# Decoder layer on one core: the last pair's projection between its value products, batched one-hots in the routing, bank sums ahead of the token list, first row turnings among the shared products

## The chip, the cores and the metric

One core of a Trainium2 chip runs the whole layer as one program. The metric is device microseconds from start to end of an execution. The core has five engines, each with its own instruction queue that runs in order: TensorE (PE), VectorE (DVE), ScalarE (ACT), GpSimd (POOL) and SyncE (SP, which here only starts DMAs). They meet at semaphores alone.

## The reference

1,024 tokens (4 batches of 256) of width 256 pass three parts; each adds to the stream x.

```
x = x + attn1(layernorm(x))                      # 16 heads of 16, causal
x = x + experts_by_token_id(layernorm(x))        # 4 experts, chosen by the token's id
h = layernorm(x)
a = rmsnorm(h, ln1_w)                            # part 3
q, k, v = a @ q_w.T, a @ k_w.T, a @ v_w.T        # 16 heads of 128, causal, scale 192**-0.5
hid = h + attention(q, k, v) @ o_w.T
x2 = rmsnorm(hid, ln2_w)
p = softmax(x2 @ gate_w.T)                       # 16 experts
w, i = top_k(p, 4);  w = w / sum(w)
routed = sum over k of w[k] * (silu(x2 @ g[i_k].T) * (x2 @ u[i_k].T)) @ w2[i_k].T    # inner 176
shared = (silu(x2 @ sg.T) * (x2 @ su.T)) @ sd.T  # inner 352
x = x + hid + routed + shared
```

## The kernel before

**Third attention.** The 16 heads go in 8 pairs. A pair `p` has 8 slots `u = 4a + b` (head `a` of the pair, batch `b`); `n = 8p + u` counts them. In slot `u`, TensorE's queue holds the scores of unit n+1, fills (the next head's q, k, v products), the value product of unit n-1 (`pe_pv3`, it needs the turned probabilities copied by ScalarE and VectorE, `act_pt3`, `dve_pt3`) and the turning of unit n. Most large products are done as three matmuls of split operands (high and low parts, `matmul3`, L226), so each operand has a "high" cast on ScalarE and a "low" subtraction on VectorE or GpSimd. The outputs of a head are copied out in two halves (`act_o3`, `dve_o3`; half 0 holds batches 0 and 1). `outputs3` says in which slot. The output projection of a pair (`pe_wo3`) has four groups of 12 matmuls, one for each 256 tokens, in banks `F_PS`, which VectorE adds to `acc` (`dve_wo3`). For all pairs but the last it is run in the next pair's slots; for the last pair it stands behind everything:

```
            pe_pv3(pe, 4 * H3 - 1, PAIRS - 1, 1, 3, H3 - 1, False)
            pe_wo3(pe, PAIRS - 1, BEFORE + PER_PAIR * (PAIRS - 1) + 4)
            pe_moe(pe)
```

In the last pair's slots, ScalarE and GpSimd also cast the first routed experts' weights (slots 1 to 3) and the shared expert's (slots 4 to 6).

**Norm and logits.** ScalarE squares `acc` by tiles, GpSimd makes the reciprocal root (`rms_gpsimd`), VectorE makes `h` (`dve_apply4`), SyncE stores h to DRAM as `x2d`, TensorE turns it (`transposes`, L197), ScalarE copies it twice (`act_hT4`, `hT_scalar`), and TensorE makes the logits (`pe_logits`, L1598).

**Shared expert and routing.** The shared expert has 6 steps `v` (two halves of the tokens by three chunks): `pe_gate_up` (12 matmuls of 512 columns), `act_silu`, `dve_shared`, `pe_down` (8 matmuls, L1588). The routing stands between them on VectorE: probabilities, the four largest, a prefix count on TensorE (`pe_prefix`), the place of each token in the list of its expert (`dve_places`), and for each of the four choices `k` two one-hot tensors (`dve_rows`): `Vk` (128 x 8 x 47, slot of the token, times a value) and `Rk` (128 x 8 x 128, row in the slot). `pe_list` multiplies them (8 products of 47 columns, L1620); their sum is the list of tokens, which `dve_tokens` turns into `tok` and `dst`. `Vk` lies in `acc`'s space and `Rk` in that of hT and h, so a step may start only when `acc` (by `dve_residual`) or h (stored) is done with. Order is written out by hand in `pe_moe`, `dve_moe` and `act_moe`.

**Routed slots.** 47 slots of 128 rows. GpSimd gathers the rows of slot s from `x2d` (L1468, ring of 8), TensorE turns them (`pe_turn`, L1631), ScalarE and VectorE copy them, then gate-up with the slot's expert (`G`, high and low), silu and product, turning, down product (L1661), ScalarE's copy into a ring of 4 (L1528), and GpSimd scatters the rows to `yb` (L1473). GpSimd's queue is ten gathers, then in turn gather s+10 and scatter s-3. Gather s waits for the turning of slot s-8. The 16 experts' low parts (`expert_low`, L1462, 128 x 704) are 5 on GpSimd ahead of the slots, 2 on VectorE ahead of them and 9 on VectorE in the slots. After the last scatter, `yb` is read back and summed with the weights.

SyncE's queue: experts 0 to 2, then 3 to 6 after the last pair's fills, the down weights `wd` (2.8 MB) after the last value product, the two stores of `x2d`, experts 7 to 10 after the last projection, experts 11 to 15 after the sixth shared down product.

Of the kernel before, what the change touches and what calls it, by code (L numbers as in the profile page):

```python
# [51 lines left out]
POOL_E = 5  # L52
RING = 8
TAIL_WARM = 36
MASKED = -1.0e30
# [4 lines left out]
RT_TOK = RT_POS + 2 * TOPK + 3  # L60
RT_ESL = RT_TOK + 4


def decoder_kernel(nc, x_in, tok_in, ctxT_in, wqT_in, wkT_in, wvT_in, woT_in, vec_in, bo_in, ffn_qk_in, ffn_v_in, ffn_o_in,
                   gate_in, sh_in, gu_in, wd_in, ln2_in, cst_in, ident_in, tri_in, out):
    with ExitStack() as ctx:
# [1091 lines left out]
        def pe_wo3(pe, p, fe_before, banks=range(4)):  # L1158

            pe.wait_ge(s_wol, p + 1)  # L1160
            pe.wait_ge(s_ol3, 4 * (p + 1))
            for g in banks:
                if g < 2:
                    pe.wait_ge(s_fe3, 2 * (fe_before - 1 + g))
                else:
                    pe.wait_ge(s_acc, 4 * p + g - 1)
# [19 lines left out]
        def pe_slot3(pe):  # L1186
            def slot(p, a, b, u, first, last, end):
# [19 lines left out]
                pe_transpose3(pe, n, u % 2, first and u < 2)  # L1207
            return slot
# [23 lines left out]
        def outputs3(p, a, b, first, last):  # L1232
# [3 lines left out]
            if last:  # L1236
                return {0: [(2 * p, 0, 0)], 2: [(2 * p, 0, 1), (2 * p + 1, 1, 0)]}.get(b, [])
# [12 lines left out]
        def act_slot3(act):  # L1250
            def slot(p, a, b, u, first, last, end):
# [7 lines left out]
                for head, a2, half in outputs3(p, a, b, first, last):  # L1259
                    if last and (a, b) == (1, 2):  # L1260
# [8 lines left out]
                if a == 1 and b == 2:  # L1269
                    act_wo3(act, p, first)  # L1270
                if last and 1 <= u < 4:
                    act_expert_high(act, u - 1)
                if last and 4 <= u < 4 + SC:
                    act_shared_high(act, u - 4)
            return slot

        def dve_slot3(dve):
            def slot(p, a, b, u, first, last, end):
# [12 lines left out]
                for head, a2, half in outputs3(p, a, b, first, last):  # L1291
                    dve_o3(dve, head, a2, half)
            return slot

        def pool_slot3(pool):
            def slot(p, a, b, u, first, last, end):
# [6 lines left out]
                if a == 1 and b == 2:  # L1303
                    pool_wo3(pool, p)
                if last and 1 <= u < 4:
                    expert_low(pool, u - 1, s_glp)
                if last and 4 <= u < 4 + SC:
                    pool_shared_low(pool, u - 4)
# [82 lines left out]
        s_glp = sem("s_glp")  # L1391
# [84 lines left out]
        def pool_moe(pool):  # L1476
            for e in range(3, POOL_E):
                expert_low(pool, e, s_glp)
# [51 lines left out]
        def act_diag(act, g, k):  # L1530

            act.wait_ge(s_rt, RT_ESL + 7)
            act.activation(diag[:, g, k, :], ident[:, :], ACT.Copy, scale=wkk[:, 2 * g + 1, k:k + 1]).then_inc(s_gh, 1)

        def act_moe(act):
# [6 lines left out]
            for v in range(2 * SC):  # L1542
                act_silu(act, v)
                if 1 <= v < 1 + len(GROUPS[2]):
                    act_expert_high(act, GROUPS[2][v - 1])
# [71 lines left out]
        def pe_list(pe, k):  # L1617
            pe.wait_ge(s_rt, RT_POS + 2 * k + 2)
# [5 lines left out]
        def pe_turn(pe, s):  # L1624
# [3 lines left out]
            else:  # L1628
                pe.wait_ge(s_am, 2 * SC - 1 + s)
# [34 lines left out]

# [550 lines left out]
```

## Time and profile before

| | |
|---|---|
| median of 3 runs (lowest, highest) | 673.27 us (669.9, 673.46) |
| profiled execution, span | 675.55 us, 673.7 us |
| busy: PE, DVE, ACT, POOL | 92%, 63%, 52%, 48% |
| mean granted clock of TensorE | 0.967 of 2.4 GHz |

Times in the rows count from the span's start, in us. A line number of a helper (L226, `matmul3`) stands for all its callers; the tiles' names tell them apart. The granted clock is a share of 2.4 GHz; 0.50 is 1.2 GHz, and a value between is a stretch that holds both. In the chain of waits, "issue" is time in which the engine waited for nothing that the profile shows. A number in brackets at the end of a timeline's row is idle time of the engine ahead of it, with what ended it.

### The profile page before, as it was taken

How to read it: one execution, taken by the hardware profiler on the slowest of the kernel's cores; microseconds unless marked ns; L12 is line 12 of the kernel's file. 1: busy time of each engine (PE TensorE's matmuls, PEld its weight loads, DVE VectorE, ACT ScalarE, POOL GpSimd, SP SyncE). 2: the span in 40 equal slices, each digit the busy share in tenths (PEclk: the TensorE clock that was granted, in tenths of full speed). 3: DMA queues.
4: the chain of work that ended last, by engine and by line, in shares of the span. 5: the costliest groups of instructions: out<-in, count | busy, mean ns of one | idle time of the engine just before them, and what ended most of it. 6: DMA issues, size and time to landing. Idle time of an engine off the chain costs nothing.

```text
span 673.7 us, 13478 instructions
## 1 busy us (share of the span) xinstructions
PE 620.3 (92%) x4132; PEld 541.5 (80%) x4132; DVE 424.4 (63%) x1134; ACT 350.5 (52%) x1120; POOL 324.0 (48%) x402
## 2 busy tenths in 40 slices
PE   8789888999889999999999999995879899999897
PEld 5567667888779999999999999995768799877775
DVE  4685887878556666666666666663694684444324
ACT  2567878443466656564756566665520165443330
POOL 7888887005433333333343433365102577777740
PEclk9899999999999999999999999996787999999899
DMA  5998930210000101020202020222820523333318
GB/s 172 219 135 209 157 36 1 83 65 2 1 0 3 62 1 62 0 62 0 62 0 62 0 62 0 79 90 49 189 84 21 158 93 101 104 102 103 102 65 310
DMA packets 27985, 52.36 MB, mean 78 GB/s; under 512 B 4235, under 2 KB 16011, under 8 KB 27851
## 3 DMA queue, kind: packets, MB, share of 16 engines
q1 hardware_dynamic: 22371, 38.79, 22.4%
q0 software_dynamic: 4512, 12.33, 5.7%
q10 hardware_dynamic: 1056, 0.66, 0.5%
q8 instruction: 25, 0.41, 0.3%
q14 instruction: 21, 0.17, 0.1%
HBM read 39.31 MB, written 12.45 MB: 77 GB/s over the span
## 4 chain that ended last, share of the span: by engine, by line
PE 63%; DVE 11%; POOL 8%; issue 6%; ACT 5%; DMA 5%; SPq 1%; ACTq 1%; DVEq 0%; POOLq 0%
PE bank L226 40%; PE bank L1661 4%; PE bank L1137 2%; DMA yb<-hx,dst 2%; POOL yb L1473 2%; PE bank L505 2%; DMA hx<-yb 2%; PE bank L1220 2%; POOL p L626 2%; PE bank L1588 2%; PE bank L1128 1%; POOL h L1468 1%; PE bank L488 1%; DMA x<-in 1%; PE bank L521 1%
## 5 line engine op out<-in xcount | busy, mean ns | idle before, releaser
L279 POOL TENSOR_TENSOR p_sb<-p_sb,prec 128x256 f32<-128x256 f32 (+1 forms) x128 | 62.3, 508 | 139.4 <-DVE prec L273 139.4
L266 ACT ACTIVATE p_sb<-bank,nmax 128x256 f32<-128x256 f32 x64 | 30.4, 475 | 89.3 <-DVE nmax L259 89.3
L616 ACT ACTIVATE p<-bank,nmax 128x256 f32<-128x256 f32 (+1 forms) x128 | 52.6, 426 | 20.8 <-DVE nmax L608 20.1
L626 POOL TENSOR_TENSOR p<-p,rec 128x512 f32<-128x512 f32 x48 | 50.2, 1055 | 17.2 <-DVE rec L621 16.9
L1473 POOL DMA_INDIRECT yb<-hx,dst x47 | 47.7, 1015 | 20.1 <-issue 11.6
L226 PE MATMUL bank<-hTh,w3h 128*128 128x512 f32 x128 | 53.0, 414 | 1.8 <-DVE hTl L220 1.8
L226 PE MATMUL bank<-G,xTh 128*128 x188 | 51.5, 357 | 0.0
L273 DVE RECIPROCAL prec<-psum_ 128x2 f32<-128x2 f32 x64 | 10.6, 166 | 63.3 <-ACT p_sb L268 63.3
L226 PE MATMUL bank<-hTh,w3l 128*128 128x512 f32 x128 | 50.4, 394 | 0.0
L226 PE MATMUL bank<-hTl,w3h 128*128 128x512 f32 x128 | 50.0, 391 | 0.0
L1661 PE MATMUL bank<-wd,hx 88*128 x188 | 49.2, 385 | 0.0
L1468 POOL DMA_INDIRECT xg<-x2d,tok x24 | 23.4, 975 | 50.5 <-DVE tok L1826 38.3
L1528 ACT ACTIVATE hx<-bank 128x256 f32<-128x256 f32 x47 | 18.1, 385 | 52.1 <-DMA yb<-hx,dst 38.8
L608 DVE TENSOR_REDUCE nmax<-bank 128x2 f32<-128x512 f32 (+1 forms) x48 | 32.7, 682 | 13.9 <-PE bank L491 13.8
L1873 DVE COPY hx<-bank 88x256 f32<-88x256 f32 x47 | 19.8, 421 | 34.0 <-PE bank L1653 33.0
L226 PE MATMUL bank<-wv3h,hTh 128*128 128x256 f32 x128 | 37.3, 292 | 2.8 <-DVE k3l L1107 2.8
L226 PE MATMUL bank<-wo3h,ctxTh 128*128 128x256 f32 x128 | 38.3, 299 | 1.5 <-issue 1.5
L226 PE MATMUL bank<-wo3l,ctxTh 128*128 128x256 f32 x128 | 36.8, 288 | 0.0
L226 PE MATMUL bank<-wo3h,ctxTl 128*128 128x256 f32 x128 | 36.8, 287 | 0.0
L505 PE MATMUL bank<-ident,p 128*128 128x128 f32 x192 | 30.5, 283 | 5.9 <-POOL p L626 5.6
L226 PE MATMUL bank<-wv3l,hTh 128*128 128x256 f32 x128 | 35.6, 278 | 0.0
L226 PE MATMUL bank<-wv3h,hTl 128*128 128x256 f32 x128 | 35.6, 278 | 0.0
(263 smaller groups left out, 2113.7 us busy)
## 6 DMA issues: line engine op xcount, KB each, us to landing
Gf<-in SPq DMA_DIRECT2D x16, 352.0 KB, 5.3
qk<-staged SPq DMA_DIRECT2D x36, 128.0 KB, 6.7
staged<-qk SPq DMA_DIRECT2D x8, 512.0 KB, 9.7
w<-in SPq DMA_DIRECT2D x16, 256.0 KB, 3.2
wd<-in SPq DMA_DIRECT2D x1, 2816.0 KB
wv<-in SPq DMA_DIRECT2D x9, 256.0 KB, 3.6
wo<-in SPq DMA_DIRECT2D x9, 256.0 KB, 2.6
hx<-yb SPq DMA_DIRECT2D x2, 1024.0 KB, 10.2
```

The costliest lines, as they stand in the source:

```text
L226: mm = pe.matmul(out, lhs[a], rhs[b], start=(start and i == 0), stop=(stop and i == 2), skip_group_check=check)
L266: act.activation(p_sb[:, k, 0:256], S_PS[k][:, 0:256], ACT.Exp, bias=nmax[:, k, 0:1], accum_out=sums[0]).then_inc(u.ex, 1)
L279: pool.tensor_tensor(p, p, r.to_broadcast(p.shape), ALU.mult).then_inc(u.pn, 1)
L505: mm = pe.transpose(ps[:, (k * job.keys // P + kb) * P:(k * job.keys // P + kb + 1) * P], job.probs(n % 2)[:, k, kb * P:(kb + 1) * P], ide ...
L608: dve.tensor_reduce(nmax1[:, n % 2, job.stats], job.scores(), AX.X, ALU.max, negate=True).then_inc(job.nm, 1)
L616: act.activation(job.probs(n % 2)[:, k, :], job.scores()[:, k, :], ACT.Exp, bias=nmax1[:, n % 2, i:i + 1], accum_out=sums1[:, n % 2, i:i + ...
L626: pool.tensor_tensor(p, p, rec1[:, n % 2, job.stats].unsqueeze(2).to_broadcast(p.shape), ALU.mult)\
L1468: pool.indirect_dma_start(RG[s % RING], None, x2d[:, :], bass.IndirectOffsetOnAxis(ap=tok[:, s:s + 1], axis=0))\
L1473: pool.indirect_dma_start(yb[:, :], bass.IndirectOffsetOnAxis(ap=dst[:, s:s + 1], axis=0), ysb[:, s % 4, :], None)\
L1528: act.activation(ysb[:, s % 4, :], YS_PS[s % 2][:, 0:D], ACT.Copy).then_inc(s_oe3, 1)
L1661: mm = pe.matmul(YS_PS[s % 2][:, 0:D], aT[:, s % 2, c, :], wd[:, bass.ds(e, 1), c, :].rearrange("p a n -> p (a n)"), start=(c == 0), stop= ...
L1873: dve.tensor_copy(aT[:, s % 2, :, :], AT_PS[s % 2][0:DC, 0:2 * P].rearrange("p (c k) -> p c k", c=2))\
```

## The change

- Last pair: `pe_wo3` group 0 stands between the turning of the last unit and its value product, group 1 behind that product, groups 2 and 3 after them. Groups 0 and 1 wait for three output halves and not for four.
- Last pair: the copy of head 15's half 0 moves from slot 6 to slot 7, the wo3 casts from slot 6 to slot 5, the shared casts from slots 4 to 6 to slots 1 to 3. The routed experts' high casts leave the slots: one behind the last output, the others behind the silus of the shared expert (`EARLY_HIGH`).
- All 16 low parts of the routed experts are on VectorE: three ahead of the slots, then one in each of slots 0 to 12.
- `dve_rows`: two batched comparisons and one batched product in place of 16 operations.
- `residual` 0 to 3 move: 0 and 1 behind `dve_apply4`, 2 and 3 among the one-hot steps. `hT_vector` of the second half stands ahead of the second logits. The first bank sums (`dve_shared_out`) and the slots' experts stand ahead of `dve_tokens`.
- `pe_turn` 0 and 1 stand among the last shared products and wait for silu 4 and 5; the wait for the last bank sums moves to the first slots' down products.
- 7 and 6 matmuls of zeros (bf16, 512 columns) stand ahead of the two turnings of h.
- The order of the down and list products changes: before gu0 gu1 prefix gu2 dn0 list0 list1 gu3 list2 list3 dn1 dn2 gu4 dn3 gu5 dn4 dn5 turn0 turn1; after gu0 gu1 prefix dn0 gu2 dn1 list0 gu3 list1 dn2 list2 list3 dn3 gu4 gu5 turn0 dn4 turn1 dn5.

The diff, cut to its core (the count bases of `s_rt` move with the third operation of each row step):

```diff
-POOL_E = 5
+EARLY_HIGH = {0: (1, 2), 1: (3, 4), 2: (5, 6), 3: (7, 8, 9, 10)}
+AHEAD = 3
...
+HEAD_WARM = (7, 6)
...
-RT_TOK = RT_POS + 2 * TOPK + 3
-RT_ESL = RT_TOK + 4
+RT_ESL = RT_POS + 3 * TOPK + 4
+RT_TOK = RT_ESL + 3
...
-        def pe_wo3(pe, p, fe_before, banks=range(4)):
+        def pe_wo3(pe, p, fe_before, banks=range(4), outputs=4):
...
-            pe.wait_ge(s_ol3, 4 * (p + 1))
+            pe.wait_ge(s_ol3, 4 * p + outputs)
...
-                if g < 2:
+                if g < 2 and fe_before is not None:
...
+                if end:
+                    pe_wo3(pe, p, None, range(0, 1), outputs=3)
...
         def pe_pv3(pe, n, p, a, b, head, nofree):
...
-                return {0: [(2 * p, 0, 0)], 2: [(2 * p, 0, 1), (2 * p + 1, 1, 0)]}.get(b, [])
+                return {0: [(2 * p, 0, 0)], 2: [(2 * p, 0, 1)], 3: [(2 * p + 1, 1, 0)]}.get(b, [])
...
         def act_o3(act, head, a, i):
...
-                    if last and (a, b) == (1, 2):
+                    if last and a == 1 and b >= 2:
...
-                if a == 1 and b == 2:
+                if a == 1 and b == (1 if last else 2):
...
-                if last and 1 <= u < 4:
-                    act_expert_high(act, u - 1)
-                if last and 4 <= u < 4 + SC:
-                    act_shared_high(act, u - 4)
+                if last and 1 <= u < 1 + SC:
+                    act_shared_high(act, u - 1)
...
         def dve_slot3(dve):
...
+                if last and u == 1:
+                    dve.wait_ge(s_lb, DONE + 32)
+                    dve.tensor_copy(lowb[:, :], cst[:, C_LOWB:C_LOWB + P]).then_inc(s_lb, 1)
+                    dve.memset(onesb[:, :], 1.0).then_inc(s_lb, 1)
...
         def pool_slot3(pool):
...
-                if a == 1 and b == 2:
+                if a == 1 and b == (1 if last else 2):
...
-                if last and 1 <= u < 4:
-                    expert_low(pool, u - 1, s_glp)
-                if last and 4 <= u < 4 + SC:
-                    pool_shared_low(pool, u - 4)
+                if last and 1 <= u < 1 + SC:
+                    pool_shared_low(pool, u - 1)
...
         def pool_moe(pool):
-            for e in range(3, POOL_E):
-                expert_low(pool, e, s_glp)
...
-                if 1 <= v < 1 + len(GROUPS[2]):
-                    act_expert_high(act, GROUPS[2][v - 1])
+                for e in EARLY_HIGH.get(v, ()):
+                    act_expert_high(act, e)
...
-                pe.wait_ge(s_am, 2 * SC - 1 + s)
+                pe.wait_ge(s_gs, 2 * SC - 1 + s)
...
         def pe_slot_gate_up(pe, s, e):
...
-            if s >= 2:
-                pe.wait_ge(s_am, SHARES + s - 1)
-            if s < POOL_E:
-                pe.wait_ge(s_glp, s + 1)
-            elif s < E3:
-                pe.wait_ge(s_gld, s - POOL_E + 1)
+            pe.wait_ge(s_am, SHARES + s - 1)
+            if s < E3:
+                pe.wait_ge(s_gld, s + 1)
...
+            else:
+                pe.wait_ge(s_yx, ADDED)
...
+        def pe_zeros(pe, times, ps):
+            for i in range(times):
+                pe.matmul(ps[:, :], zb[:, 0:P], zb[:, :], start=True, stop=True, skip_group_check=True)
         def pe_moe(pe):
...
+                pe_zeros(pe, HEAD_WARM[g], bank[0])
...
+            pe_down(pe, 0)
...
-            pe_down(pe, 0)
+            pe_down(pe, 1)
...
+            pe_gate_up(pe, 3)
...
-            pe_gate_up(pe, 3)
+            pe_down(pe, 2)
...
-            pe_down(pe, 1)
-            pe_down(pe, 2)
+            pe_down(pe, 3)
...
-            pe_down(pe, 3)
...
+            pe_turn(pe, 0)
...
+            pe_turn(pe, 1)
...
-            pe.wait_ge(s_yx, ADDED)
-            pe_turn(pe, 0)
-            pe_turn(pe, 1)
...
-            for i in range(TAIL_WARM):
-                pe.matmul(SUM_PS[1][:, :], zb[:, 0:P], zb[:, :], start=True, stop=True, skip_group_check=True)
+            pe_zeros(pe, TAIL_WARM, SUM_PS[1])
...
-            for t in range(NT):
-                one = dve.tensor_scalar(Vk[k][:, t, :], cst[:, C_SLOT:C_SLOT + SLOTS], pb[:, t, k:k + 1], val[:, t, k:k + 1],
-                                        ALU.is_equal, ALU.mult)
-            one.then_inc(s_rt, 1)
-            for t in range(NT):
-                one = dve.tensor_scalar(Rk[k][:, t, :], cst[:, C_ROW:C_ROW + P], rowf[:, t, k:k + 1], None, ALU.is_equal)
-            one.then_inc(s_rt, 1)
+                dve.wait_ge(s_yx, 3)
+            dve.tensor_tensor(Vk[k], cst[:, C_SLOT:C_SLOT + SLOTS].unsqueeze(1).to_broadcast([P, NT, SLOTS]),
+                              pb[:, :, k:k + 1].to_broadcast([P, NT, SLOTS]), ALU.is_equal).then_inc(s_rt, 1)
+            dve.tensor_tensor(Rk[k], cst[:, C_ROW:C_ROW + P].unsqueeze(1).to_broadcast([P, NT, P]),
+                              rowf[:, :, k:k + 1].to_broadcast([P, NT, P]), ALU.is_equal).then_inc(s_rt, 1)
+            dve.wait_ge(s_rt, RT_POS + 3 * k + 1)
+            dve.tensor_tensor(Vk[k], Vk[k], val[:, :, k:k + 1].to_broadcast([P, NT, SLOTS]), ALU.mult).then_inc(s_rt, 1)
...
         def dve_tokens(dve):
...
         def dve_moe(dve):
...
-            for g in range(2):
-                dve_logits(dve, g)
+            dve_logits(dve, 0)
+            hT_vector(dve, n4, 1)
+            dve_logits(dve, 1)
...
-            hT_vector(dve, n4, 1)
...
+            dve_shared(dve, 1)
...
+            dve_residual(dve, 2)
...
-            dve_shared(dve, 1)
...
+            dve_shared(dve, 2)
...
-            dve_shared(dve, 2)
-            dve_tokens(dve)
...
+            dve_residual(dve, 3)
...
+            dve_tokens(dve)
+            dve_weights(dve)
+            expert_low(dve, 0, s_gld)
...
-            dve_weights(dve)
+            expert_low(dve, 1, s_gld)
...
-            for e in range(POOL_E, 7):
-                expert_low(dve, e, s_gld)
+            dve_turned(dve, 0)
+            expert_low(dve, 2, s_gld)
+            dve_turned(dve, 1)
...
-            dve_turned(dve, 0)
-            dve_turned(dve, 1)
...
-                if 7 + s < E3:
-                    expert_low(dve, 7 + s, s_gld)
+                if AHEAD + s < E3:
+                    expert_low(dve, AHEAD + s, s_gld)
...
-            for e in GROUPS[1]:
-                act_expert_high(act, e)
+            act_expert_high(act, 0)
...
-            pe_wo3(pe, PAIRS - 1, BEFORE + PER_PAIR * (PAIRS - 1) + 4)
+            pe_wo3(pe, PAIRS - 1, None, range(1, 2), outputs=3)
+            pe_wo3(pe, PAIRS - 1, None, range(2, 4))
...
+            dve_wo3(dve, PAIRS - 1, range(0, 1))
...
-            dve.wait_ge(s_lb, DONE + 32)
-            dve.tensor_copy(lowb[:, :], cst[:, C_LOWB:C_LOWB + P]).then_inc(s_lb, 1)
-            dve.memset(onesb[:, :], 1.0).then_inc(s_lb, 1)
-            for g in range(4):
+            for g in range(1, 4):
...
-                if g < 2:
-                    dve_residual(dve, g)
...
-                if not g:
-                    dve_residual(dve, 2)
-            dve_residual(dve, 3)
+            for g in range(2):
+                dve_residual(dve, g)
```

## Rows read from the trace of the kernel before

**Rows 1.** The page's costliest groups: ... | busy us, mean ns | idle us, releaser.

```profile
L1528 ACT ACTIVATE hx<-bank 128x256 f32<-128x256 f32 x47 | 18.1, 385 | 52.1 <-DMA yb<-hx,dst 38.8
```

**Rows 2.** Stretches: us, busy time of the five engines, granted clock, DMA share, GB/s.

```profile
458.00:461.40 3.40, 0.09 (x1) 0.01 (x1) 2.08 (x5) 2.62 (x7) 2.47 (x4) 0.89 0.00 0
...
467.50:475.00 7.50, 7.47 (x48) 7.27 (x48) 3.61 (x7) 4.53 (x14) 4.13 (x4) 0.77 0.70 144
...
482.00:487.00 5.00, 5.00 (x35) 4.96 (x35) 1.78 (x5) 2.56 (x5) 0.00 (x0) 0.74 0.82 178
...
503.20:512.00 8.80, 8.79 (x30) 7.64 (x30) 7.70 (x34) 0.00 (x0) 0.00 (x0) 0.51 0.01 2
```

**Rows 3.** The chain of waits, last pair to last projection: start us, us, what.

```profile
458.33 0.97 ACT ctxTh L1242 x2
459.31 0.52 ACT wo3h L1072
459.83 0.52 ACT wsh L1493
...
466.03 1.46 issue
467.49 7.50 PE bank L226 x48
```

**Rows 4.** The same chain, norm, turning and logits.

```profile
479.06 0.49 DVE h L1720
479.60 2.52 PE bank L197 x8
482.12 4.81 PE bank L1598 x32
```

**Rows 5.** The same chain, products of the shared expert and lists.

```profile
512.06 3.64 PE bank L1620 x32
...
523.53 1.73 PE bank L1588 x8
525.26 2.76 PE bank L226 x12
```

**Rows 6.** Timeline of VectorE: start us, us, engine, line, operation, count, idle before.

```profile
496.52 1.80 DVE L1813 TENSOR_SCALAR acc<-cst,pb,val 128x47 f32<-128x47 f32 x8
498.24 1.65 DVE L1817 TENSOR_SCALAR hT<-cst,rowf 128x128 f32<-128x128 f32 x8
...
516.20 0.19 DVE L1826 TENSOR_SCALAR tok<-tok 128x47 int32<-128x47 int32 x1
...
525.98 0.68 DVE L1851 TENSOR_TENSOR prod<-key,srt 128x512 f32<-128x512 f32 x1
...
542.00 0.88 DVE L1462 TENSOR_TENSOR G<-Gf,G 128x704 fp32r<-128x704 f32 x1
```

**Rows 7.** Timeline of GpSimd, gathers and scatters.

```profile
517.28 1.22 POOL L1468 DMA_INDIRECT xg<-x2d,tok  x1 [38.25 <-DVE tok L1826]
...
533.76 0.94 POOL L1468 DMA_INDIRECT xg<-x2d,tok  x1 [5.56 <-PE bank L1631]
...
542.09 1.60 POOL L1468 DMA_INDIRECT h<-x2d,tok  x1 [1.33 <-PE bank L1631]
544.00 1.71 POOL L1473 DMA_INDIRECT yb<-hx,dst  x1 [0.30 <-issue]
...
630.90 0.99 POOL L1473 DMA_INDIRECT yb<-hx,dst  x1 [0.30 <-issue]
...
642.06 0.97 POOL L1473 DMA_INDIRECT yb<-hx,dst  x1 [1.31 <-ACT hx L1528]
644.33 0.97 POOL L1473 DMA_INDIRECT yb<-hx,dst  x1 [1.30 <-ACT hx L1528]
...
653.25 0.97 POOL L1473 DMA_INDIRECT yb<-hx,dst  x1 [0.31 <-issue]
```

**Rows 8.** Timeline of TensorE near the end.

```profile
651.93 7.93 PE L1707 MATMUL bank<-zb 128*128 128x512 bf16 x36
```

More of the change, by code:

```diff
@@ L1390, in decoder_kernel @@
         s_gh = sem("s_gh")
-        s_glp = sem("s_glp")
         s_gld = sem("s_gld")
@@ L1530, in act_diag @@
         def act_diag(act, g, k):
-            act.wait_ge(s_rt, RT_ESL + 7)
+            act.wait_ge(s_rt, RT_TOK + 7)
             act.activation(diag[:, g, k, :], ident[:, :], ACT.Copy, scale=wkk[:, 2 * g + 1, k:k + 1]).then_inc(s_gh, 1)
@@ L1617, in pe_list @@
         def pe_list(pe, k):
-            pe.wait_ge(s_rt, RT_POS + 2 * k + 2)
+            pe.wait_ge(s_rt, RT_POS + 3 * k + 3)
             for t in range(NT):
@@ L1830, in dve_slot_experts @@
             dve.tensor_tensor(ends[:, :], base[:, :], nslot[:, :], ALU.add).then_inc(s_rt, 1)
-            dve.wait_ge(s_rt, RT_TOK + 1)
+            dve.wait_ge(s_rt, RT_ESL - 3)
             dve.tensor_tensor(ecmp[:, :, :], ends[0:1, :].unsqueeze(1).to_broadcast([1, SLOTS, E3]),
@@ L1834, in dve_slot_experts @@
                .then_inc(s_rt, 1)
-            dve.wait_ge(s_rt, RT_TOK + 2)
+            dve.wait_ge(s_rt, RT_ESL - 2)
             dve.tensor_reduce(esum[:, :], ecmp[:, :, :], AX.X, ALU.add).then_inc(s_rt, 1)
-            dve.wait_ge(s_rt, RT_TOK + 3)
+            dve.wait_ge(s_rt, RT_ESL - 1)
             dve.tensor_scalar(esl[:, :], esum[:, :], float(E3 - 1), None, ALU.min).then_inc(s_rt, 1)
@@ L1842, in dve_weights @@
             dve.scalar_tensor_tensor(chosen[:, :, :], left[:, :, :], 0.0, pr[:, :, :], ALU.is_lt, ALU.mult).then_inc(s_rt, 1)
-            dve.wait_ge(s_rt, RT_ESL + 1)
+            dve.wait_ge(s_rt, RT_TOK + 1)
             dve.tensor_reduce(sums[:, :], chosen[:, :, :], AX.X, ALU.add).then_inc(s_rt, 1)
-            dve.wait_ge(s_rt, RT_ESL + 2)
+            dve.wait_ge(s_rt, RT_TOK + 2)
             dve.reciprocal(sums[:, :], sums[:, :]).then_inc(s_rt, 1)
-            dve.wait_ge(s_rt, RT_ESL + 3)
+            dve.wait_ge(s_rt, RT_TOK + 3)
             dve.tensor_tensor(chosen[:, :, :], chosen[:, :, :], wide(sums[:, :]), ALU.mult).then_inc(s_rt, 1)
@@ L1852, in dve_weights @@
                               ALU.is_equal).then_inc(s_rt, 1)
-            dve.wait_ge(s_rt, RT_ESL + 5)
+            dve.wait_ge(s_rt, RT_TOK + 5)
             dve.tensor_tensor(eq, eq, chosen[:, :, :].unsqueeze(2).to_broadcast(shape), ALU.mult).then_inc(s_rt, 1)
-            dve.wait_ge(s_rt, RT_ESL + 6)
+            dve.wait_ge(s_rt, RT_TOK + 6)
             dve.tensor_reduce(wkk[:, :, :], eq, AX.X, ALU.add).then_inc(s_rt, 1)
```

## The prediction, made before the changed kernel was run

> **What bounds the kernel now.** I read the page first. TensorE is the busiest engine of the span, so its work and its clock matter most, but late in the kernel another engine is the one that others wait for: ScalarE's copies of the routed results sat idle 52.1 us, 38.8 of them until a scatter had landed [rows 1]. Then I cut the part that the diff touches into stretches and read TensorE's busy time beside the granted clock [rows 2]. TensorE stands almost still from 458.0 to 461.4 us, and the clock then falls from 1.00 to 0.50 (2.4 to 1.2 GHz). It is at 0.77 over the projection, low again in the logits' stretch (0.74 over 482 to 487), and at half rate in the stretch with the list products (0.51), where TensorE was busy throughout. The chain of waits says what TensorE waited for, and the timelines of VectorE and GpSimd give durations and the order of their queues.
>
> The chain reads thus. The last pair's ScalarE queue holds two output copies, the wo3 cast and a wsh cast ahead of the copy of the next turned probabilities [rows 3]; TensorE waits for that copy. After the last value product it waits again, 1.46 us, for the last output's low part, and only then starts the 48 matmuls of the projection [rows 3]. Then come the norm, its turning and the logits [rows 4], the shared expert mixed with the routing [rows 5], the one-hots on VectorE [rows 6], and 94 gathers and scatters on GpSimd [rows 7]. From 544.00 to 630.90 GpSimd issues one scatter and one gather in turn, without a pause beyond its own issue time, 33 pairs in 86.9 us, 2.63 us each. That is the pace of the routed slots: TensorE, which does one in 2.27 us where it sets the pace (642.06 to 644.33), waits through ScalarE for the scatters [rows 1, 7]. The question is thus when GpSimd's first gather starts, how soon its queue runs without a pause, and what stretches it.
>
> **Part 1, end of the last pair.** Before, TensorE's idle time from 458.0 ends at 461.4 [rows 2]. The wo3 cast goes to slot 5, the wsh cast to slot 3, and one of the two output copies behind the turned copy: 1.6 us leave ScalarE's queue ahead of it [rows 3]. The first output's low part stays ahead of it on VectorE (0.69), so I take 1.1 us: the product starts at 460.3. In slot 5 the cast waits for the last group of the previous projection, which TensorE issues ahead of that slot's value product; the exponential ahead of the cast ends later, so I cost the move at nothing (1.4 us, one group, if that cover is gone). The 48 matmuls took 7.50 us at a mean clock of 0.77 [rows 2, 3], so a group of 12 is 1.44 us at full clock and 2.6 at half. Group 0 now fills the time in which TensorE waited for the last turned copy, group 1 the 1.46 us for the last output. The idle stretch shrinks only from 3.4 to 2.3 us, so I still expect one dip, ending sooner because TensorE is then busy without a gap. With one dip of about 3.4 us, at half rate, the order is: value product to 461.5, turning to 462.2, group 0 to 464.5, last product to 465.4, then three groups of 1.44: end at 469.7 instead of 475.0. Gain 5.3. Bounds: 6.5 with no dip, 1.0 with half clock throughout.
>
> **Part 2, norm to logits.** From the projection's end the second `h` tile group comes after 4.05 us in both kernels, through VectorE, ScalarE and GpSimd, and the turning ended 7.1 us after it, the logits 11.9 us after it [rows 4]. 13 matmuls of zeros (0.22 us each at full clock, 36 took 7.93 near the end [rows 8]) fill TensorE's pauses; they cost nothing while they end before `h` comes, at most 0.3 us in front of the first turning, which nobody waits for. If they hold the clock, turning ends with the last `h` at 6.2, and 32 logit matmuls take 4.81 x 0.74 = 3.6 us: 9.8 instead of 11.9. Gain 2.1; bound 0. The residual sums leave VectorE's queue ahead of `h`, which came out of its wait for rstd anyway.
>
> **Part 3, logits to token list.** Count from the logits' end, L (486.9 before). At full clock a gate-up product is 2.76 us, a down product 1.73, a list product 3.64 / 2 = 1.82 [rows 5]. Places ended at L+9.6 and start after the prefix behind two gate-ups, so this stays. One row step cost 1.72 + 1.64 = 3.36 us of VectorE (8 + 8 instructions) [rows 6]. A two-input operation of 512 columns took 0.68 us and of 704 columns 0.88, so 1.04 us for each 1,000 columns and 0.15 fixed [rows 6]. The batched step is 376 + 1,024 + 376 columns: 0.54 + 1.21 + 0.54 = 2.3 us. That is 1.07 less, four times 4.3. VectorE's new queue is: shared 0.65, rows 2.3, residual 0.7, rows 2.3, rows 2.3, shared 0.65, rows 2.3, shared 0.65, residual 0.7, two bank sums 1.3, slot experts 2.2, tokens 0.6. From L+9.8 that is L+26.5. TensorE's new order ends the last list at L+24.4 if the clock holds, so VectorE sets the tokens, and emptying the banks plus the slot experts ahead of them costs 1.4 us of it. Before it was 516.39, L+29.5 [rows 6]. Gain 3.0. Bounds: 4.4 if the tokens came straight behind the last list, and 0 if the clock dips twice (1.7 us each).
>
> **Part 4, tokens to first scatter.** Before: first gather 0.9 us behind the tokens, eight gathers, then 5.56 us of idle time until the first row turning, 1.35 and 1.33 us for the next ones, scatter 0 at 544.00, 27.6 us behind the tokens [rows 7]. After: turns 0 and 1 stand among the shared products, at about L+31.7 and L+33.6, before GpSimd needs them (it reaches gather 8 at L+38). So it runs 14 gathers at 1.27 us (0.97 and 0.30 of issue) [rows 7] without a pause: 0.9 + 17.8. TensorE's first slot starts at L+35.8, and slot output 0 is ready in time. To this come stretched issues: the issue of 542.09 took 1.60 us while VectorE's cast of 542.00 ran, against 0.97 [rows 6, 7]. All sixteen low parts are now on VectorE, three ahead of the slots and thirteen in them; before it had eleven, nine of them in the slots. In the trace four of the nine casts inside the slots met an issue so, 0.65 us each (the one at 544.00 is another): 0.29 us per cast. Up to scatter 0 that is ten casts' worth with the weights' operations, 3.2 us. Sum 21.9 instead of 27.6. Gain 5.7; bounds 8.9 (no stretch) and 2.3 (each meets one). GpSimd loses its five casts, which it did while it had nothing else to issue; TensorE waited for none of them: nothing. If that cover is gone the price is VectorE's 0.88 us for each, once ahead of the slots.
>
> The GPSIMD Engine Reference (section 8, Key points) of the Trainium skill says that GpSimd shares its SBUF interface with VectorE and contends with VectorE instructions that have two SBUF inputs; the cast is one, and the trace agrees in four of nine cases. Taken for every cast, that rule is rival (e).
>
> **Part 5, slots.** 33 pairs as before, with eight casts in place of six: 87.5 instead of 86.9, a loss of 0.6. From scatter 33 to the last took 22.35 us and the rest of the kernel 20.4 [rows 7]; both stay. SP's last expert loads wait for the same count of down products and come nearer to the first slots; what they delay on ScalarE is hidden behind GpSimd's pace.
>
> **Sum.** 5.3 + 2.1 + 3.0 + 5.7 - 0.6 = 15.5 us off a span of 673.7. One more dip in the list products at even odds takes 0.8. The profiled run took 675.55, the median is 673.27; 673.3 - 14.7 = **658.5**.
>
> **Rivals.** (a) The forecast, 0.52, 653 to 664. (b) TensorE's clock stays at half: the dip at 461 lasts through the projection (-4.3), the zeros do not hold it (-2.1), two more dips lie in the lists (-2.6 beyond the 0.8): 667.5. For it speaks that 467.5 to 475 and 503 to 512 are low in the trace although TensorE was busy [rows 2]; 0.14. (c) TensorE's shorter way is worth more than I count, the issues rarely meet a cast and no dip comes: 5.3 to 6.5 in part 1, 3 us in part 4, 0.8: 653; 0.15. (d) The batched one-hots are not shorter, because a broadcast operand slows them: 4.3 us later tokens, 662.8. Against it: the 0.68 us row has two broadcast operands [rows 6]; 0.06. (e) Each of 16 casts stretches an issue by 0.65: 10.4 instead of 4.6, 664.3; 0.08. (f) Slower: the small-column list products spread among the others keep the clock at 1.2 GHz through all shared products. 34 us of TensorE's work at full clock become 64, 29 us more; with the other gains kept, the kernel is slower by 14, 687. It turns at 15 us of added time, that is half clock over 30 of these us. Against it: the gate-up product of 525.26 ran at full clock, 12 matmuls in 2.76 us, close behind list and down products [rows 5]; 0.05.
>
> Chances: faster by over 0.5% (3.4 us, about what this measurement can tell from no change) 0.94, within 0.02, slower 0.04. The range takes (c) with 4 us below and (b) above: 649 to 668.
>
> **What would show it.** The projection's first 12 matmuls between the last turning and the last value product; its end near 470; the logits' end near 479.5; one-hot operations of 0.54 and 1.21 us; tokens at about 506; GpSimd without idle time from the first gather; scatter 0 near 528; scatter 33 near 615. Wrong would be: the first value product not before 461, a granted clock of 0.50 over most of the shared products, tokens behind the last down product, or slots paced by TensorE at 2.27 us.

## The result, and the profile after

| | before | after |
|---|---|---|
| median (lowest, highest), 4 runs each | 673.37 us (669.9, 674.96) | 652.66 us (651.88, 655.19) |
| ratio of the times, 95% interval | | 0.9716 (0.9687 to 0.9745) |
| profiled execution, span | 675.55, 673.7 us | 652.61, 650.7 us |
| mean granted clock | 0.967 | 0.991 |
| busy: PE, DVE, ACT, POOL | 92%, 63%, 52%, 48% | 94%, 65%, 54%, 48% |

The kernel is 20.7 us faster; 14.7 were forecast. In the ratios here and below, two runs at a lower clock than the rest (683.27 us of before, 704.92 us of turns_behind_2) are left out. The page's group that answers to [rows 1] is unchanged, so the routed slots run as they did, and the gain lies ahead of them and in the kernel's last part:

```profile
L1529 ACT ACTIVATE hx<-bank 128x256 f32<-128x256 f32 x47 | 18.1, 384 | 52.0 <-DMA yb<-hx,dst 39.2
```

The stretches after (us, busy time of PE, PEld, DVE, ACT, POOL, granted clock, DMA share, GB/s), beside [rows 2]:

```profile
458.00:459.00 1.00, 0.60 (x4) 0.63 (x5) 0.85 (x3) 0.00 (x0) 0.00 (x0) 0.80 0.00 0
459.00:460.00 1.00, 1.00 (x7) 1.00 (x6) 0.00 (x0) 0.00 (x0) 0.00 (x0) 0.50 0.00 0
...
462.00:463.00 1.00, 1.00 (x10) 1.00 (x10) 0.44 (x1) 0.00 (x0) 0.00 (x0) 0.99 0.00 0
...
463.00:475.00 12.00, 11.63 (x79) 8.90 (x80) 7.61 (x16) 8.08 (x24) 2.63 (x4) 1.00 0.76 176
475.00:480.00 5.00, 5.00 (x33) 4.50 (x33) 4.45 (x19) 2.88 (x5) 0.00 (x0) 1.00 0.83 177
495.00:504.00 9.00, 9.00 (x62) 8.37 (x62) 8.65 (x20) 2.51 (x4) 1.17 (x1) 1.00 0.00 1
609.00:630.90 21.90, 20.71 (x118) 17.04 (x118) 7.90 (x23) 8.20 (x25) 13.91 (x15) 1.00 0.24 88
```

One dip is left, the forecast one at 458 to 462. The projection's remainder, the logits and the list products, which [rows 2] show at 0.77, 0.74 and 0.51, run at 2.4 GHz. The chain of waits after, from the product of the last unit but one to the turnings of the rows, beside [rows 3, 4, 5]:

```profile
458.40 0.80 PE bank L228 x3
...
460.26 2.62 PE bank L228 x15
...
464.53 0.03 issue
464.56 3.12 PE bank L228 x24
...
469.63 0.41 POOL ve L185
...
471.15 1.69 DVE h L1723 x4
...
473.65 3.57 PE bank L1599 x32
...
497.67 3.50 PE bank L1621 x32
...
508.48 0.22 PE bank L1632 x2
508.70 1.73 PE bank L1589 x8
```

The 15 products of 460.26 are projection group 0 and the last value product; groups 2 and 3 (464.56) follow with 0.03 us of issue where before there were 1.46. TensorE's timeline has the idle time ahead of 458.40:

```profile
458.40 0.37 PE L228 MATMUL bank<-pt3h,v3h 128*128 128x256 f32 x1 [2.13 <-DVE pt3f L1152]
```

VectorE's timeline of one row step, and of the tokens, beside [rows 6]:

```profile
487.15 0.54 DVE L1816 TENSOR_TENSOR acc<-cst,pb 128x376 f32<-128x376 f32 x1
487.61 1.22 DVE L1818 TENSOR_TENSOR hT<-cst,rowf 128x1024 f32<-128x1024 f32 x1
488.75 0.54 DVE L1821 TENSOR_TENSOR acc<-acc,val 128x376 f32<-128x376 f32 x1
489.21 0.68 DVE L1735 TENSOR_TENSOR x<-x,acc 128x512 f32<-128x512 f32 x1
...
501.32 0.18 DVE L1825 TENSOR_TENSOR dst<-bank,cst 128x47 int32<-128x47 f32 x1
...
501.76 0.19 DVE L1829 TENSOR_SCALAR tok<-tok 128x47 int32<-128x47 int32 x1
```

GpSimd's timeline, first gather, the stretched gathers, first scatter, scatter 33 and the last one, beside [rows 7]:

```profile
502.83 1.28 POOL L1471 DMA_INDIRECT xg<-x2d,tok  x1 [31.72 <-DVE sums L1849]
504.42 0.95 POOL L1471 DMA_INDIRECT xg<-x2d,tok  x1 [0.30 <-issue]
...
518.35 1.41 POOL L1471 DMA_INDIRECT h<-x2d,tok  x1 [0.30 <-issue]
520.06 1.62 POOL L1471 DMA_INDIRECT h<-x2d,tok  x1 [0.31 <-issue]
521.99 1.00 POOL L1476 DMA_INDIRECT yb<-hx,dst  x1 [0.30 <-issue]
...
609.65 0.99 POOL L1476 DMA_INDIRECT yb<-hx,dst  x1 [0.30 <-issue]
...
630.00 0.97 POOL L1476 DMA_INDIRECT yb<-hx,dst  x1 [0.30 <-issue]
```

The pauses of 5.56 and 1.33 us ahead of the ninth and later gathers [rows 7] are gone.

Some more rows of before are needed for the comparison. TensorE's timeline shows how it came to the list stretch:

```profile
499.94 2.13 PE L1620 MATMUL bank<-acc,hT 128*128 128x47 f32 x16 [2.43 <-DVE hT L1817]
```

Behind that stretch, its last two lists (512.06 to 515.70 [rows 5]) and the down products after them ran without a gap, and the clock fell once more:

```profile
512.00:515.70 3.70, 3.70 (x34) 3.70 (x33) 0.00 (x0) 1.28 (x2) 0.00 (x0) 0.94 0.00 0
515.70:520.40 4.70, 4.70 (x17) 3.87 (x17) 1.27 (x4) 0.00 (x0) 2.51 (x3) 0.68 0.09 28
```

The chain of waits has GpSimd's first operation of the norm:

```profile
476.93 1.01 POOL ve L183
```

And one stretch shows the clock of before near the end:

```profile
634.00:640.00 6.00, 6.00 (x28) 5.30 (x29) 2.20 (x7) 2.16 (x7) 3.57 (x5) 0.72 0.23 91
```

### The profile page after: what moved, and what is told of

Read it like the earlier page. It is cut to its first block, busy times and chain, and to the rows that moved or that the text cites. A ratio compares the mean times of both kernels' runs of the same rounds, so it can differ in the third digit from the quotient of the medians.

```text
span 650.7 us, 13445 instructions
## 1 busy us (share of the span) xinstructions
PE 608.7 (94%) x4135; PEld 531.4 (82%) x4145; DVE 422.9 (65%) x1087; ACT 349.3 (54%) x1120; POOL 315.3 (48%) x397
## 4 chain that ended last, share of the span: by engine, by line
PE 61%; DVE 11%; POOL 10%; issue 6%; ACT 6%; DMA 5%; another core or an unknown queue 1%; SPq 1%; ACTq 1%; DVEq 0%; POOLq 0%
PE bank L228 40%; PE bank L1661 3%; POOL yb L1476 3%; PE bank L1139 2%; DMA hx<-yb 2%; PE bank L507 2%; POOL p L628 2%; PE bank L1589 2%; DMA yb<-hx,dst 2%; PE bank L1224 2%; POOL xg L1471 1%; PE bank L1130 1%; POOL h L1471 1%; DVE ctxTl L1251 1%; PE bank L523 1%
## 5 line engine op out<-in xcount | busy, mean ns | idle before, releaser
L618 ACT ACTIVATE p<-bank,nmax 128x256 f32<-128x256 f32 (+1 forms) x128 | 52.5, 424 | 20.1 <-DVE nmax L610 19.5
L228 PE MATMUL bank<-G,xTh 128*128 x188 | 50.0, 348 | 0.0
L1471 POOL DMA_INDIRECT xg<-x2d,tok x24 | 24.7, 1028 | 38.7 <-DVE sums L1849 31.7
L1870 DVE TENSOR_TENSOR hx<-hx,bank 128x176 f32<-128x176 f32 x47 | 15.6, 332 | 31.1 <-ACT hx L1523 30.9
```

The source lines that it names most:

```text
L228: mm = pe.matmul(out, lhs[a], rhs[b], start=(start and i == 0), stop=(stop and i == 2), skip_group_check=check)
L618: act.activation(job.probs(n % 2)[:, k, :], job.scores()[:, k, :], ACT.Exp, bias=nmax1[:, n % 2, i:i + 1], accum_out=sums1[:, n % 2, i:i + ...
L1471: pool.indirect_dma_start(RG[s % RING], None, x2d[:, :], bass.IndirectOffsetOnAxis(ap=tok[:, s:s + 1], axis=0))\
L1870: dve.tensor_tensor(amx[:, s % 2, :], sg[:, s % 2, :], GS_PS[s % 2][:, INNER:GW], ALU.mult).then_inc(s_am, 1)
```

## The experiments

Each kernel is the changed one with one edit (combo has two), timed beside the kernel before on the same chip. They ran in three sessions; lowest and highest are over all runs of a kernel.

| session | kernel | median us (lowest, highest) | ratio to before (95%) |
|---|---|---|---|
| 1 | before | 673.22 (670.05, 683.27) | |
| 1 | control | 653.4 (652.81, 654.45) | 0.9719 (0.9684, 0.9753) |
| 1 | old_slots | 653.49 (651.9, 653.71) | 0.9709 (0.9673, 0.9745) |
| 1 | no_zeros | 655.62 (654.05, 657.48) | 0.9739 (0.9704, 0.9774) |
| 1 | old_rows | 657.85 (657.59, 658.93) | 0.9783 (0.9748, 0.9817) |
| 2 | before | 690.97 (689.36, 696.0) | |
| 2 | proj_behind | 678.47 (677.24, 681.76) | 0.9831 (0.9791, 0.987) |
| 2 | turns_behind | 675.56 (673.46, 677.43) | 0.9768 (0.973, 0.9806) |
| 2 | no_slot_casts | 675.91 (673.94, 678.38) | 0.979 (0.975, 0.983) |
| 2 | ring8 | 674.47 (672.69, 677.28) | 0.9771 (0.9731, 0.9811) |
| 3 | before | 691.09 (688.0, 693.73) | |
| 3 | control_2 | 676.9 (674.91, 678.03) | 0.9793 (0.9766, 0.9819) |
| 3 | combo | 674.74 (673.32, 677.63) | 0.9772 (0.9742, 0.9803) |
| 3 | turns_behind_2 | 673.86 (672.14, 704.92) | 0.9754 (0.9725, 0.9783) |
| 3 | no_slot_casts_2 | 677.12 (675.43, 679.55) | 0.9813 (0.9786, 0.9841) |

In sessions 2 and 3 every kernel took longer, before by 17.8 us and the changed one by 23.5. The change was thus worth 20 us in session 1 and 14 in session 3. In the profiles the extra time lies in the routed slots: the first gather comes at 503.28 in control_2 (502.37 in control), the last scatter at 655.30 (629.39). The stages ahead of the slots can therefore be compared between sessions; the slots only within one. Session 2 had no control.

**control** is the changed kernel again, to see what repeats.

> The changed kernel once more, as the measure for the others of this call. Span 650 to 653.5 us, ratio to before 0.969 to 0.975; one clock dip of about 3.4 us near 459, none in the shared products, tokens near 502, scatter 0 near 522, scatter 33 near 609.7.

It repeats in time. But the turning of unit 62, the last but one of the last pair, comes at 455.43 in control, 455.78 in the first profile, 456.21 in control_2, 456.86 in proj_behind and 459.27 in no_zeros, though nothing ahead of it differs. So a stage's start moves by up to 3.8 us from profile to profile, and a difference of that size between the starts of a stage in two profiles is no effect. The length of one stretch repeats far better: from unit 0's turning in the last pair to unit 62's it is 20.02 us in control (435.41 to 455.43), 20.03 in the first profile and 20.04 in no_zeros.

**old_slots** puts the shared casts back into slots 4 to 6:

```diff
-                if last and 1 <= u < 1 + SC:
-                    act_shared_high(act, u - 1)
+                if last and 4 <= u < 4 + SC:
+                    act_shared_high(act, u - 4)
```

(the same for GpSimd's `pool_shared_low`).

> The changed kernel with the shared expert's casts back in slots 4 to 6 of the last pair. Theory: these casts stood in front of the turned copies there, so the last value products come 1.5 to 2.5 us later and so does everything behind them; the kernel is 2 us slower than the control. Rival: the 1.9 us by which slot 7 came earlier than I forecast is owed to the routed experts' casts leaving slots 1 to 3; then this costs under 0.5 us.

The median did not move, and my theory for the unforecast part of part 1's gain fell. In the trace the stretch from unit 0's turning to the projection's end is 0.5 us longer than in control (32.32 and 31.80 us). The rival named the routed experts' casts, which left slots 1 to 3. No run puts them back, but from unit 0's turning to unit 62's the changed kernel is only 0.5 us shorter than before (20.03 and 20.55), so both moves of casts together can't be worth more there.

**no_zeros** takes the 13 matmuls of zeros out.

```diff
-HEAD_WARM = (7, 6)
+HEAD_WARM = (0, 0)
```

> The changed kernel without the 13 matmuls of zeros. Theory: the zeros hold TensorE's clock; without them it falls to 0.50 over the second turning and most of the logits, which end 2 to 2.5 us later, and the kernel is 2 to 2.5 us slower than the control. Rival: h now comes soon enough and the clock stays; under 0.5 us.

Its chain and its stretches:

```profile
475.54 2.12 PE bank L199 x7
477.66 4.18 PE bank L1599 x32
```

```profile
475.00:477.00 2.00, 1.78 (x6) 1.17 (x7) 2.00 (x6) 0.15 (x1) 0.00 (x0) 0.60 0.70 165
477.00:479.50 2.50, 2.50 (x17) 2.50 (x16) 1.16 (x3) 2.25 (x5) 0.00 (x0) 0.64 1.03 250
```

The dip is back in the stage where [rows 2] have it, and the logits take 4.18 us and not 3.57. Of the twelve other profiles of the changed kernel and its variants, all with the zeros, none has a granted clock below 1.00 between 468 and 500 us. From the last 24 projection products to the logits' end it is 13.84 us (468.01 to 481.85), in control 12.66 (464.08 to 476.74): 1.2 us. The medians differ by 2.2, and the intervals of the two ratios overlap; the other 1.0 is not assigned.

**old_rows** goes back to 16 operations for each row step (the `dve.tensor_scalar` lines of the diff).

> The changed kernel with the one-hots made by 16 operations a step as before (the third signal of a step is given with the second). Theory: a step takes 3.36 us instead of 2.06, VectorE sets the tokens, which come 4.5 to 6 us later; the clock may dip in the lists for 1.7 more; the kernel is 5 to 7 us slower than the control. Rival: TensorE's list products set the tokens and hide VectorE's steps; then under 1.5 us.

A row step takes 3.27 us of VectorE (487.74 to 491.01) and not 2.06. Four of them make 4.8; the way from the logits' end to the first gather grew from 25.63 to 30.50 us, 4.9, and the medians by 4.45. In this kernel TensorE waits for VectorE once more, 0.39 us at 504.8, behind its last two lists, and its clock falls there:

```profile
504.00:508.50 4.50, 4.11 (x14) 3.32 (x14) 4.22 (x14) 0.00 (x0) 0.19 (x1) 0.62 0.00 0
```

**proj_behind** puts all four projection groups behind the last value product (VectorE's additions follow):

```diff
-                if end:
-                    pe_wo3(pe, p, None, range(0, 1), outputs=3)
...
-            pe_wo3(pe, PAIRS - 1, None, range(1, 2), outputs=3)
-            pe_wo3(pe, PAIRS - 1, None, range(2, 4))
+            pe_wo3(pe, PAIRS - 1, None, range(0, 4))
```

> The changed kernel with all four groups of the last projection behind the last value product, as before. Theory: TensorE waits again about 1.1 us for the last turned copy and 1.5 us for the last output, and the clock stays at 0.50 for one stretch more; from the turning of unit 62 to the projection's end it takes 2.6 to 4.5 us longer, and the kernel is as much slower than the control. Rival: the gain in this stretch came from the shorter queue of casts alone; then under 1 us.

Its chain has before's wait again, to the hundredth [rows 3]:

```profile
463.20 1.46 issue
464.66 7.33 PE bank L228 x48
```

From the turning (456.86) to the projection's end it is 15.1 us, in control 11.8 (455.43 to 467.20): 3.4 us, and the same 3.4 to the first gather (50.35 and 46.94). That includes the clock, which stays at 0.50 until 467 us and in control until 461. The median lies 2.6 to 4.0 us above those of the three other variants of its session.

Its profile shows something else that control's does not, a dip right behind the last two lists (502.04 to 505.54), with TensorE busy throughout:

```profile
502.00:505.00 3.00, 3.00 (x30) 3.00 (x29) 2.90 (x6) 0.00 (x0) 0.00 (x0) 1.00 0.01 3
505.00:509.00 4.00, 4.00 (x14) 3.34 (x14) 3.72 (x12) 0.00 (x0) 1.49 (x2) 0.57 0.00 0
```

**turns_behind**, and once more **turns_behind_2**, put the first two row turnings behind the shared products, where they wait for the last bank sums (VectorE's queue is reordered to match).

```diff
-            pe_turn(pe, 0)
             pe_down(pe, 4)
-            pe_turn(pe, 1)
             pe_down(pe, 5)
...
+            pe.wait_ge(s_yx, ADDED)
+            pe_turn(pe, 0)
+            pe_turn(pe, 1)
```

> The changed kernel with the first two row turnings behind the last shared product and the bank sums, as before. Theory: TensorE stands still 1.6 us for the bank sums, the clock may fall, and GpSimd's ninth gather waits for the turning; scatter 0 comes 3 to 4 us later behind the first gather, the kernel is 3 to 4 us slower than the control. Rival: GpSimd sets the pace from its first gather, and its ten gathers hide the later turnings; under 1 us.

> The first two row turnings behind the last shared product and the bank sums, as before the change, now beside a control. Theory: scatter 0 comes 3 to 4 us later behind the first gather than the control's 19.1 and the kernel is 3 to 4 us slower. Rival: GpSimd's ten gathers hide the later turnings; under 1 us.

GpSimd's ninth gather does wait again, in turns_behind_2:

```profile
513.98 0.94 POOL L1471 DMA_INDIRECT xg<-x2d,tok  x1 [1.29 <-PE bank L1632]
```

That is 1.29 us where before had 5.56 [rows 7]. The other 4.3 us have another cause: the last shared product ends 9.1 us behind the first gather here (511.69 and 502.58), and 14.2 us in before (531.47 and 517.28). So most of that pause went because less shared work is left when the tokens are ready, and not because of the place of the turnings. From first gather to scatter 0 it is 22.15 us and in control_2 22.6, where 3 to 4 us more were expected, and the medians do not put it behind control_2 (673.86 and 676.9). What the moved turnings are worth in the slots of session 1 isn't shown.

**no_slot_casts** and **no_slot_casts_2** leave out the 13 low casts inside the slots; their experts' routed products take the high part in place of the low one.

> The changed kernel without the 13 low casts in the slots; the low part of each routed gate-up weight is replaced by its high part in the products, the count of matmuls is the same. Theory: the seven stretched issues of GpSimd (3.9 us together over 0.97 each) come from these casts; the issues go to 0.97 to 1.0, scatter 33 comes 84.5 to 85.5 us behind scatter 0 instead of 87.7, the kernel is 3 to 4 us faster than the control. Rival: the stretches come from the transfers of that time; then nothing changes.

> The kernel without the 13 low casts in the slots (high parts of the weights stand in for the low ones in the products), now beside a control. Theory: GpSimd's issues of 1.3 to 1.7 us in the slots go to 0.97 to 1.0, scatter 33 comes 84.5 to 85.5 us behind scatter 0 instead of 87.7, the kernel is 3 to 4 us faster than the control. Rival: the stretches come from the transfers of that time; no change.

The page's groups of GpSimd's issues, no_slot_casts_2:

```profile
L1476 POOL DMA_INDIRECT yb<-hx,dst x47 | 46.3, 985 | 24.2 <-ACT hx L1529 13.8
L1471 POOL DMA_INDIRECT xg<-x2d,tok x24 | 23.5, 978 | 46.2 <-DVE sums L1851 31.7
```

and control_2:

```profile
L1476 POOL DMA_INDIRECT yb<-hx,dst x47 | 47.6, 1014 | 27.5 <-ACT hx L1529 17.1
L1471 POOL DMA_INDIRECT xg<-x2d,tok x24 | 24.8, 1031 | 45.9 <-DVE sums L1849 31.7
```

Without casts the means fall to the 0.97 to 0.99 us of an unstretched issue: the stretches come from the casts. No time came of it (677.12 and 676.9, where 3 to 4 us were expected), so in the slots of sessions 2 and 3 the issues do not set the pace.

**ring8** gives the scatters eight buffers and not four, for the 52.0 us of idle time in the changed kernel's group of [rows 1] (the rest of the edit finds room and semaphores for them).

```diff
-            if s >= 4:
-                act.wait_ge(s_sc[s % 4], 16 * (s // 4))
+            if s >= YR:
+                act.wait_ge(s_sc[s % YR], 16 * (s // YR))
```

> The changed kernel with eight buffers for the slots' outputs instead of four. Theory: GpSimd paces the slots through the ring; with four buffers TensorE may lead by four slots only, so when the gathers are over eight slots are left at TensorE's 2.27 us. With eight it leads by more, the last scatter comes 16.6 to 17.5 us behind scatter 33 instead of 20.3, the kernel is 3 to 4 us faster than the control. Rival: TensorE reaches its 2.27 us pace nowhere in the middle, for the gathers or VectorE hold it; then nothing changes.

The waits for scatters are no longer what idles ScalarE's copies (38.6 us, 21.6 of them for TensorE), but in control_2, with four buffers, they aren't either (45.0 us, 37.6 for TensorE). From scatter 33 to the last it is 24.4 us (expected 16.6 to 17.5); control_2 has 29.8, but turns_behind with four buffers has 25.7. No gain is shown: against before it has 0.9771, control_2 0.9793, intervals that overlap.

**control_2** and **combo** ran together. combo is ring8 with nine matmuls of zeros in TensorE's wait ahead of unit 62's value product:

```diff
+                    if end:
+                        pe.wait_ge(s_acc, 4 * p)
+                        pe_zeros(pe, VALUE_WARM, F_PS[1])
```

> The changed kernel again, as the measure for the others of this call. In the call before, every kernel, the one before the change too, was 17 to 20 us longer in the routed slots alone, and no control stood beside it. Ratio to before 0.969 to 0.976.

> Eight buffers for the slots' outputs, and nine matmuls of zeros in front of the value product of unit 62. Theory: TensorE's lead in the slots grows to eight, the last scatter comes 16.6 to 17.5 us behind scatter 33 instead of 20.3 (-3 to -4 us); the zeros hold the clock over the last pair's end, which saves 1.5 to 1.9 us between the turning of unit 62 and the projection's end. Together 4.5 to 6 us faster than the control. Rivals: the tail does not change, because TensorE is held by something other than the ring (-1.5 alone); the zeros only delay the value product (0 to +0.5).

The stretches of control_2 around its wait:

```profile
457.00:458.00 1.00, 0.00 (x0) 0.00 (x0) 0.68 (x2) 1.00 (x3) 0.77 (x2) 1.00 0.00 0
...
459.00:460.00 1.00, 1.00 (x7) 1.00 (x7) 0.29 (x1) 0.00 (x0) 0.00 (x0) 0.68 0.00 0
460.00:461.00 1.00, 1.00 (x7) 1.00 (x6) 0.09 (x1) 0.38 (x1) 0.00 (x0) 0.50 0.00 0
```

and of combo:

```profile
458.00:459.00 1.00, 1.00 (x5) 0.48 (x5) 0.47 (x2) 1.00 (x5) 0.54 (x1) 1.00 0.00 0
...
460.00:461.00 1.00, 0.93 (x9) 0.96 (x9) 0.52 (x1) 0.00 (x0) 0.00 (x0) 1.00 0.00 0
461.00:462.00 1.00, 1.00 (x11) 1.00 (x10) 0.34 (x1) 0.38 (x1) 0.00 (x0) 1.00 0.00 0
```

With zeros in the wait the last dip is gone. All twelve other profiles of the changed kernel and its variants have it. From turning to the last 24 projection products it is 7.23 us (457.44 to 464.67) and not 8.79 (456.21 to 465.00): 1.6 us, as expected. The last scatter comes 26.6 us behind scatter 33, where 16.6 to 17.5 were expected. The medians (674.74 and 676.9) go the same way as the 1.6 us, but the intervals of the ratios overlap. In session 1 it wasn't timed.

## Why the prediction was right, point by point

The spans differ by 23.0 us, the medians by 20.7, 6.0 more than forecast; the profiled execution of before lies 2.2 above its median. The time, 652.66 us, is within the range of 649 to 668, but just below the 653 to 664 that the forecast itself named as (a).

| step | forecast | measured in the profiles |
|---|---|---|
| 1, last pair to projection end | 5.3 | 7.3 (475.0 to 467.7) |
| 2, norm, turning, logits | 2.1 | 2.4 |
| 3, logits to tokens | 3.0 | 4.7 |
| 4, tokens to scatter 0 | 5.7 | 7.6 |
| 5, scatter 0 to 33 | -0.6 | -0.8 (87.66 and 86.9) |
| scatter 33 to the last | 0 | 2.0 (20.35 and 22.35) |
| last scatter to the end | 0 | -0.25 |
| another dip, even odds | -0.8 | none came |

**Part 1: right over the stretch that it counted.** The order and the single dip are as predicted, the wait ahead of the value product 2.13 us against 2.3. From unit 62's turning to the projection's end it is 17.4 us before (457.60 to 474.99) and 11.9 after (455.78 to 467.68): 5.5 for a forecast 5.3. proj_behind shows 3.4 of it for the moved groups; the rest goes with the shorter queue of ScalarE (a wait of 2.13 us and not 3.33 ahead of the value product) and is argued. Of the 1.8 us beyond it, 1.3 was there at unit 0's turning in the last pair, ahead of every change of order (435.75 in place of 437.05); starts of equal kernels spread by more. The other 0.5 lies in the pair's slots, and old_slots gives back half of it there (20.28 us and not 20.02).

**Part 2: right**, 9.5 us from the projection's end to the logits' end against a forecast 9.8. The second `h` came 0.6 us sooner than the 4.05 that I kept, because `ve` took 0.41 us and not 1.01. That the zeros are what holds the clock is shown by no_zeros, whose dip no profile with the zeros has.

**Part 3: mechanism right, 1.7 us short.** The durations of the batched operations were nearly exact (0.54, 1.22, 0.54 us for 0.54, 1.21, 0.54). Their sum was not the queue's time: each starts before the one ahead has ended, 0.46 and 1.14 us after its start. A step thus takes 2.06 us and not 2.3, and the same holds for the operations between. VectorE's list ends with `dst` at 501.32, 0.14 us behind the last list product (501.18): the bound "tokens straight behind the last list", not the 1.4 us of VectorE's own that I forecast. old_rows shows the batched steps alone to be worth 4.9 us (4.3 forecast), as much as the whole of part 3. The dip in the lists, forecast at even odds, did not come; that was partly luck. The stretches of before [rows 2] show 503.2 to 512 at half rate with TensorE busy, and TensorE had stood for 2.43 us ahead of its first list product (499.94), a wait that the new kernel lacks. But a wait is not the only thing that goes ahead of such a dip. In before the clock fell again at the end of 32 list products (515.7), and in proj_behind at the end of the same 32 (505 to 509), both times with TensorE busy throughout. In the changed kernel 32 of them at 497.67 ran at 1.00 and nothing fell behind them. Of the twelve profiles with the batched steps only proj_behind's has this dip; why it comes there is open. It lies behind the lists and so does not delay the tokens.

**Part 4: no pause, as forecast, but only in small part for the reason given.** No pause is left in 14 gathers. The text put that down to the turnings among the shared products; turns_behind_2 leaves 1.29 of the 5.56 us to them and the rest to the shorter shared work behind the tokens, which the forecast's times contained (the turnings at L+31.7 and L+33.6) but its words did not. I forecast 3.2 us of stretched issues ahead of scatter 0. Beyond 14 issues of 1.27 us there are 1.4: 1.1 in the gathers of 518.35 and 520.06, and 0.3 in the first one, which took 1.22 in before too [rows 7]. Up to 545 us seven issues are stretched, 4.0 us together (4.6 forecast for all 16 casts), while 16 casts run. no_slot_casts ties them to the casts; the GPSIMD Engine Reference (section 8, Key points) of the Trainium skill names the contention, and the trace agrees, for seven of sixteen casts. Meeting a cast is not enough: the issues of 514.59 and 530.49 ran beside casts (514.56 and 530.74) and took 0.94 and 1.00 us. Rival (e), every cast and 10.4 us, fell.

**Part 5: right** (87.66 us, 87.5 forecast). The 2.0 us of the tail I had left at zero. Before had a clock of 0.72 over 634 to 640, and the changed kernel 1.00 over the whole tail. A dip in before's one profile was thus part of its span, and nothing in the change was made to remove it. The first profile and the four of session 1 have tails of 20.1 to 20.4 us; whether before always has its dip isn't known, since only one of its runs was profiled.

**The rivals.** (b) fell: one dip, not four. (d) and (f) fell in the profile after: the durations are as computed, and 495 to 504 is at full clock. (c) names the measured time (653 and 652.66). Its conditions came half true: no dip in the lists, fewer stretched issues; but its gain in part 1 was not that of a missing dip, since the dip came, and it did not have the overlap on VectorE nor the tail. That its number is the measured one is luck.

**Open.** What slows the routed slots by 17 to 24 us in sessions 2 and 3. The stretch of 560 to 590 us, control and control_2:

```profile
560.00:590.00 30.00, 29.32 (x172) 25.08 (x173) 14.08 (x39) 12.57 (x44) 22.74 (x24) 1.00 0.31 100
```

```profile
560.00:590.00 30.00, 25.09 (x144) 20.77 (x143) 10.16 (x30) 11.99 (x40) 19.24 (x21) 1.00 0.26 88
```

TensorE, VectorE and GpSimd all do less in the same time at an unchanged clock, and the waits are named partly as "remote" (an unknown releaser). GpSimd no longer sets the pace: between scatter 0 and scatter 33 it never pauses in control, and in control_2 it waits 13 times for over a microsecond (16.4 us), seven times for a row turning and six for an unknown releaser. The number of instruction loads (47 and 46 packets) hardly differs. None of ring8, no_slot_casts and turns_behind brought the time back. Open too is how much of the 7.6 us of part 4 each moved piece brought: no run in session 1 takes one of them back.

## What to carry to other kernels

Of the 20 us, experiments assign 3.4 to ready work put into TensorE's waits (the projection groups), 1.2 to zeros that keep its clock through a wait, and 4.9 to fewer instructions on VectorE ahead of the one point for which all wait. The other half rests on comparing two profiles. When you add up a queue of VectorE operations, take the distance of their starts in the trace, not their durations. When a stretch is at half clock although its engine is busy, look at the microseconds ahead of it before you blame the work inside: most dips here had a wait ahead of them, but two, behind 32 list products, had none. And give the length of a stretch between two events rather than the time at which it starts, since starts moved by up to 3.8 us between profiles of equal programs.

## What the runs showed of the hardware

- Successive VectorE operations overlap in the trace: 0.54 us operations start 0.46 us apart, 1.22 us ones 1.14.
- The granted clock fell behind waits of TensorE of 2.13 us (458.40) and 2.43 us (499.94, before), and did not fall when nine matmuls of zeros filled the first of them (combo). Not every wait had a dip behind it: after one of 1.22 us at 498.9 in old_rows the clock stayed at 1.00 until 504.
- It also fell without a wait: at the end of 32 list products of 47 columns in before (515.7) and in proj_behind (505), with TensorE busy throughout. The same 32 products ran at full clock in the changed kernel (497.67, 3.50 us), and nothing fell behind them. In old_rows a dip (504 to 508.5) had both ahead of it, the lists and a wait of 0.39 us.
- GpSimd's issue of an indirect transfer took 0.94 to 1.03 us, and 1.27 to 1.69 us for seven issues that ran beside a VectorE cast (up to 545 us of the first profile, its first gather of 1.28 us aside); other issues beside a cast (514.59, 530.49) were not stretched.
- The same kernel took 653.4 and 676.9 us in two sessions, all of the difference in slots that issue 94 indirect transfers, with the stages ahead of them unchanged within 1 us.
